# Second layer norm's variance taken from the first one's, and new orders of work for four of five blocks

## The reference, cut to what matters

```python
x = x + ssm(_gn(x))        # in_proj, 3x3 conv, 4 selective scans of 256 steps, 96 channels, 16 states
t = to_tokens(x)
t = t + attn(_ln_t(t))     # 12 heads of 16, causal
t = t + ffn(_ln_t(t))      # begins: h = _ln(t, g, b); attention over all tokens; MLP; 4 experts, top 2

def _ln_t(v, eps=1e-05):
    m = mean(v); s = var(v)
    return (v - m) / sqrt(s + eps)
```

## Time and profile before

| | |
|---|---|
| median of 3 runs | 740.43 us (737.93 to 743.23) |
| profiled execution, its own time | 742.85 us |
| its span | 741.1 us |
| TensorE busy | 608.1 us, 82% |
| VectorE busy | 516.4 us, 70% |
| ScalarE busy | 321.5 us, 43% |
| GpSimd busy | 201.3 us, 27% |

### The profile page before, as it was taken

How to read it: one execution, slowest core, us unless ns; L and a number is a source line. 1 busy time by engine, 2 the same in 40 slices (tenths; PEclk the granted TensorE clock), 3 DMA queues, 4 the chain that set the end, 5 groups by cost and what they waited for, 6 DMA issues and landing times. The chain is left out here.

```text
span 741.1 us, 9169 instructions
## 1 busy us (share of the span) xinstructions
PE 608.1 (82%) x3378; PEld 392.0 (53%) x3378; DVE 516.4 (70%) x986; ACT 321.5 (43%) x588; POOL 201.3 (27%) x158
## 2 busy tenths in 40 slices
PE   3899947898737689958898789867996989898897
PEld 2232225455212576645455576645465767676696
DVE  3869746868998578789997478799995465542311
ACT  2334202236353053784572345583761324672241
POOL 4449710005474201053442010153441001000000
PEclk9999968689768799878999789889999999999999
DMA  6375940348772002386750004575620000000000
GB/s 130 40 178 145 278 141 0 44 99 206 185 188 60 11 0 38 80 200 155 178 134 0 22 0 57 144 187 147 181 63 11 0 2 1 0 1 11 1 1 11
DMA packets 26642, 61.70 MB, mean 83 GB/s; under 512 B 4928, under 2 KB 12752, under 8 KB 26608
## 3 DMA queue, kind: packets, MB, share of 16 engines
q1 hardware_dynamic: 26608, 61.26, 34.8%
HBM read 53.52 MB, written 3.54 MB: 77 GB/s over the span
## 5 line engine op out<-in xcount | busy, mean ns | idle before, releaser
L1106 PE MATMUL pd<-w_dn,act 128*128 128x192 f32 x480 | 87.2, 336 | 5.5 <-ACT act L1872 3.7
L1992 POOL TENSOR_TENSOR state<-state,C_rows 128x1024 f32<-128x1024 f32 x24 | 69.8, 2909 | 62.5 <-DVE state L1491 40.6
L1106 PEld LDWEIGHTS pd<-w_dn,act 128*128 128x128 f32 x480 | 80.2, 195 | 11.7 <-issue 6.3
L1090 PE MATMUL pu<-fT,w_up 128*128 128x256 f32 x180 | 61.8, 427 | 7.6 <-ACT act L1872 7.6
L1967 POOL TENSOR_TENSOR norm_rstd<-norm_var,half 128x2 f32<-128x2 f32 x20 | 14.0, 698 | 197.5 <-DVE norm_var L1304 197.5
L1872 ACT ACTIVATE act<-pu,b_up 128x256 f32<-128x256 f32 x90 | 37.7, 470 | 67.4 <-PE pu L1094 67.2
L942 PE MATMUL py<-identb 128*32 128x512 bf16 x224 | 59.1, 412 | 0.0
L1842 ACT ACTIVATE decay<-d_rows,a_neg 128x255 f32<-128x255 f32 x96 | 40.5, 498 | 11.2 <-DVE state L1491 10.3
L1092 PE MATMUL pu<-fT_high,w_up_stack 128*128 128x256 f32 x90 | 45.2, 503 | 0.0
L1032 PE MATMUL py<-state,sel 128*32 128x512 f32 x96 | 43.8, 665 | 1.6 <-POOL state L1992 1.6
L822 PE MATMUL ps<-hT,w_qkv 96*96 96x256 f32 x128 | 35.9, 444 | 9.5 <-ACT hT L1902 8.6
(11 more groups left out here) (310 smaller groups left out, 1384.6 us busy)
## 6 DMA issues: line engine op xcount, KB each, us to landing
dx_rows<-delta_x_dram SPq DMA_DIRECT2D x41, 512.0 KB, 5.2
d_rows<-delta_dram SPq DMA_DIRECT2D x36, 512.0 KB, 6.3
d_rows<-delta_x_dram SPq DMA_DIRECT2D x6, 512.0 KB, 4.8
w_dn<-exp_w_dram SPq DMA_DIRECT2D x1, 2304.0 KB
B_rows<-xdbl SPq DMA_DIRECT2D x4, 512.0 KB, 6.9
C_rows<-xdbl SPq DMA_DIRECT2D x4, 512.0 KB, 10.5
delta_x_dram<-delta_x SPq DMA_DIRECT2D x4, 384.0 KB, 3.4
w_up<-exp_w_dram SPq DMA_DIRECT2D x1, 1536.0 KB
```

Of the source, the lines that this page charges most:

```text
L1090: nc.tensor.matmul(out, w_up[:, e, hidden], fT[:, :], start=True, stop=False)
L1106: mm = nc.tensor.matmul(pd[:, WIDTH * tl:WIDTH * (tl + 1)], act[e % 2][:, m, 128 * tl:128 * (tl + 1)], w_dn[:, e, m, :], start=(m == 0), s ...
L1992: nc.gpsimd.tensor_tensor(now, now, C_rows[:, :], ALU.mult).then_inc(sc_done, 1)
```

## The change

It has two parts. In the seam, `norm(3)` loses its statistics. When rstd of norm 2 is there, VectorE forms var * rstd * rstd (which is s / (s + eps)) and adds eps, with three instructions on 128x2 numbers, and GpSimd takes the power of it while VectorE applies norm 2. h_tok is then v_tok times that number, without a shift:

```diff
-                            link(norm(2, lambda tl: x2[:, tl, :], lambda tl: v_tok[:, tl, :]))
-                            norm(3, lambda tl: v_tok[:, tl, :], lambda tl: h_tok[:, tl, :]).then_inc(h_done, 1)
+                            norm_stats(2, lambda tl: x2[:, tl, :])
+                            dve.wait_ge(rstd_done[2], 1)
+                            link(nc.vector.tensor_tensor(norm_twice[:, :], norm_mv[:, 2, :, 1],
+                                                         norm_rstd[:, 2, :], ALU.mult))
+                            link(nc.vector.tensor_tensor(norm_twice[:, :], norm_twice[:, :],
+                                                         norm_rstd[:, 2, :], ALU.mult))
+                            nc.vector.tensor_scalar(norm_var[:, 3, :], norm_twice[:, :], EPS, None,
+                                                    ALU.add).then_inc(var_done[3], 1)
+                            link(norm_apply(2, lambda tl: x2[:, tl, :], lambda tl: v_tok[:, tl, :]))
+                            dve.wait_ge(rstd_done[3], 1)
+                            for tl in range(TILES):
+                                ins = nc.vector.tensor_scalar(h_tok[:, tl, :], v_tok[:, tl, :],
+                                                              norm_rstd[:, 3, tl:tl + 1], None, ALU.mult)
+                            ins.then_inc(h_done, 1)
```

The other part is new tables for OPENING, FIRST, STEADY and LAST. SyncE's order is the same as before. In OPENING the rows of VectorE, ScalarE and GpSimd are the same too, and dummy matmuls move on TensorE. A few lines of the tables:

```diff
 FIRST "PE"
-        (0, "spread"): [("keep_busy", 19)],
-        (0, "output"): [("keep_busy", 30)],
+        (0, "context"): [("keep_busy", 6)],
+        (0, "output"): [("keep_busy", 27)],
 FIRST "POOL"
-        (1, "context"): [("y_norm",), ("split_up", 4)],
-        (1, "output"): [("y_out",), ("split_up", 5)],
+        (1, 8): [("split_up", 4), ("split_up", 5)],
+        (1, "context"): [("times_C", 11), ("y_norm",)],
+        (1, "output"): [("y_out",)],
 STEADY "PE"
-        (0, "spread"): [("ffn_up", 1, 2)],
-        (0, "output"): [("ffn_down", 1, 0), ("ffn_up", 2, 0), ("ffn_up", 2, 1)],
-        (1, "turned"): [("ffn_up", 2, 2)],
+        (0, "context"): [("ffn_turn_gates",), ("keep_busy", 15)],
+        (0, "spread"): [("ffn_bias",)],
+        (0, "output"): [("ffn_up", 1, 2), ("ffn_down", 1, 0), ("ffn_up", 2, 0), ("ffn_up", 2, 1)],
+        (1, "turned"): [("keep_busy", 17), ("ffn_up", 2, 2)],
 LAST "PE"
-        (1, "spread"): [("ffn_down", 4, 0), ("ffn_down", 4, 1)],
+        (1, "context"): [("ffn_down", 4, 0), ("ffn_down", 4, 1)],
```

More of the change, by code:

```diff
@@ L223 @@
[L223 to L229 removed]
+        (0, "turned"): [("ffn_turn", 0), ("x_turn",)],
@@ L244 @@
         (1, "projected"): [("scan", 3)],
[L245 to L254 removed]
+        (1, 0): [("scan", 4), ("scan", 5), ("ffn_add", 1)],
@@ L255 @@
+        (1, 1): [("scan", 6)],
+        (1, 3): [("scan", 7), ("scan", 8)],
+        (1, 4): [("ffn_add", 2), ("scan", 9)],
+        (1, 5): [("scan", 10)],
+        (1, 6): [("ffn_add", 3)],
+        (1, 7): [("scan", 11)],
+        (1, 10): [("y_copy",), ("y_norm",)],
+        (1, "spread"): [("y_turn",), ("ffn_add", 4), ("y_out",)],
     },
     "ACT": {
-        (0, 0): [("ffn_up", 0, 0)],
-        (0, 1): [("ffn_up", 0, 1), ("ffn_up", 0, 2), ("in_proj",), ("x_dbl", 0)],
-        (0, 3): [("x_dbl", 1)],
@@ L289 @@
+        (1, "context"): [("y_out",)],
     },
```

393 lines of the change are left out of this document (192 added, 201 removed).

## The result

The kernel after takes 746.25 us (median of 20 runs, 741.97 to 755.99), the kernel before 741.65 us in its 20 runs (737.48 to 752.83). The ratio is 1.006 with a 95% interval of 1.0042 to 1.0077: some 4.4 us slower (3.1 to 5.7). A few executions of either kernel take about 1% longer at a lower granted clock, and all ratios here are of the others. The forecast was 731.7 us, its range ended at 742. The profiled execution of after took 745.71 us, with a span of 744.0 us; that of before 742.85 and 741.1.

What follows compares the result with a forecast made beforehand. No engine alone bounds the kernel; a block is as long as a chain that changes engines. FIRST -2.2, STEADY -5.8 and LAST -0.7 make -8.7 us, from the median 740.43 to 731.7 us, range 724 to 742.

Steps and rivals of the forecast that it cites:

- The seam: Between the attentions: h_tok without second statistics is ready 1.5 us sooner; at most 6.0 us over four places.
- -0.7 at the end of the round: STEADY: the faster norm gains 0.7 us per round, between 0 and 1.5, only if ScalarE comes sooner.
- Rival A: Norm's gain hidden under ScalarE's and TensorE's queues, barrier not waiting for the store: 737.4 us, chance 0.30.
- 27 dummies: FIRST's seam: 27 instead of 30 dummies take 6.0 us, so TensorE reaches the transposes sooner: -0.65 us.
- I let the two cancel: STEADY's end: ffn_down 4 ahead of y_turn and y_out (2.1 us each part) against sums coming earlier: net zero.
- The store: STEADY's end: store lands before the sum into v, step to next block 3.8 to 1.6 us: -2.2 per round.
- -2.9 per round: STEADY: -0.7 from the norm and -2.2 from the store in each round, -5.8 over two rounds.
- forecast at -2.2: FIRST as a whole: -0.65 at the seam, -1.55 from the shifts and 0 for its first half.
- -1.55 from the shifts: FIRST's end: two shifts fall from 0.94 to 0.16 us once GpSimd's products lie earlier; bounds 0 and -1.6.
- from -2 to +2: FIRST's first half: fewer dummies free about 1 us, later in_proj delays the convolution up to 1.7 us; taken as 0.
- rival B: New dummies in STEADY stand in the way, 7.9 us exposed per round: 749.6 us, chance 0.12.
- C: Dummies at STEADY's seam keep the clock up, q, k, v matmuls 3.3 instead of 6.67 us: 726.7 us, chance 0.13.

Runs made afterwards that it cites:

- e1: Kernel before with the new seam norm alone, all tables as before; ratio 0.9992 (0.9953 to 1.0031).
- e4: Kernel before with only STEADY's round end changed: ffn_down 4 1 ahead of y_turn, ffn_add 4 ahead of y_out; ratio 0.9954 (0.9926 to 0.9981).
- e6: Kernel after with ffn_up 4 2 behind the last two sums over states in STEADY; ratio 1.0126 (1.0063 to 1.0188).
- e9: New seam and new STEADY table alone, other tables as before, with 22 of a round's 79 dummies taken out; ratio 1.0039 (1.0004 to 1.0074).
- e3: Kernel after with the 11 dummies of before put back around y_sum 11 at FIRST's end; ratio 1.0097 (1.006 to 1.0133).
- e5: Kernel after with 7 dummies of before put back in STEADY's first half; ratio 1.0095 (1.0054 to 1.0136).
- e2: Kernel after with the old double norm, all new tables kept; ratio 1.0147 (1.0087 to 1.0208).
- e7: Kernel before with the new seam and the new table for STEADY alone; ratio 1.0037 (0.9991 to 1.0084).
- e8: Kernel before with new seam, STEADY's early store and new LAST; OPENING and FIRST as before; ratio 0.9945 (0.9902 to 0.9988), 739.4 us.
- e10: Kernel after with FIRST's in_proj at its old slot, ahead of the scores; ratio 1.016 (1.0094 to 1.0226), from four runs.
- e11: Kernel after with 11 dummies in FIRST ahead of the eleventh sum over states; ratio 1.0027 (0.9991 to 1.0063).
- e12: Like e8, with FIRST's last two 64x384 GpSimd products moved between its last products with C; ratio 0.9924 (0.9897 to 0.9952), 736.46 us.
- e16: Like e12, with the old double norm; ratio 0.9946 (0.9905 to 0.9988).

## Why the prediction was wrong

**The seam** was right in its mechanism (1.65 us measured, 1.5 forecast, and the two engines don't take turns), and its "-0.7 at the end of the round" was too much for the old order: 0.1 to 0.3 in e1. Rival A described that part. In FIRST I had the 27 dummies right (6.00 us). I had not priced that 6 dummies ahead of the projection run at the lower clock: 0.5 us for the projection.

**The step that failed first** is "I let the two cancel" at the end of a STEADY round. The store gave 1.9 us, 2.2 forecast. Against it I set nothing, and two terms were there. y_copy came 1.8 and 1.5 us later behind GpSimd's last product, because TensorE reached the last sums late: its list has no wait in the 39.5 us ahead of y_copy, with 26 dummies in it. And from y_copy to the sum into v it was 0.5 us longer, with ffn_down 4 1 ahead of y_turn; by itself that move costs 1.3 to 1.7 us (e4). My reason, that the sums now come ahead of "ffn_up 4 2's neighbours", misread the tables: they stand behind ffn_up 4 2 in both, and with them ahead of it (e6) y_copy was no sooner. That the full list is what makes the sums late is argued from the windows and from e9, whose y_copy came 4.8 and 4.6 us behind the product with 13 dummies there; no ratio shows it.

From residual sum to the sum into v after is 1.0 and 1.3 us longer than before in spite of the faster norm, where I had -0.7. A round, in after less before, adds up so:

| part of a round | round 1 | round 2 | forecast |
|---|---|---|---|
| start to the seam's residual sum | +4.4 | -2.3 | 0 |
| from there to GpSimd's first product | -1.2 | -0.8 | -0.7 |
| first product to last | -0.1 | 0 | 0 |
| last product to y_copy | +1.8 | +1.5 | 0 |
| y_copy to the sum into v | +0.5 | +0.5 | 0 |
| that sum to the next block | -1.9 | -1.9 | -2.2 |

So -2.9 per round became +3.5 and -3.0. The prediction named this sign: wrong if STEADY is not shorter by 2 us per round, or if FIRST comes out longer. Both happened.

**FIRST**, forecast at -2.2, was +1.4 in this profile: the residual sum came 0.5 us later, GpSimd's first product 0.7 sooner behind it, its chain from first to last product was 1.2 longer (61.4 instead of 60.2 us, with the two weight products inside it), y_copy came 1.6 us later behind the last product, and the -1.55 from the shifts came as -1.3 (y_copy to the sum into v 11.6 us instead of 12.9). The convolution began 0.9 us later, the projection behind 6 dummies took 0.5 us longer. I had set the first half at 0 "from -2 to +2", and the longer chain and the later sum had no term. The block also moves by itself: with the new table and the new seam it was 149.7, 150.0, 150.2 and 150.3 us (after, e3, e5, e6), with the new table and the old seam 146.9 (e2); with the table of before it was 148.3, 146.2, 145.8, 147.0 and 149.9 (before, e1, e4, e7, e8). The means of these five and five are 149.4 and 147.4.

**The clock** was in rival B and C, with the wrong place. The dummies at the seam kept it up, as C said (3.69 us instead of 6.67). That is no chance of one execution: the q, k, v projection behind the seam takes 3.69 us in both rounds of all twelve profiles with the new table, and 6.55 to 6.79 in the six with the old one. The scans did not get shorter by it: from GpSimd's first product to its last 66.4 us in after, 66.5 in before. That step was right. The 1.2 and 0.8 us by which they began sooner reached GpSimd's last product and were lost behind it, on TensorE. By that reading B was right in kind, with 1.5 to 1.8 us a round where it had 7.9.

**Not foreseen at all** was TensorE's code being loaded again at the jump back to the second round: some 2.3 us on the average of the executions, and none in the six profiles with the old table. With it, a rough sum from profiles: +0.5 in OPENING, +2.0 in FIRST, -1.5 in the two rounds of STEADY from the residual sums on, -0.4 in LAST (108.7 us, the mean of after, e2, e3, e5 and e6, against 109.1), -0.3 in CLOSING (60.5 against 60.8), and +2.1 in the first halves of the two rounds, where the residual sum comes 64.1 and 61.6 us into the round (means of after, e2, e3, e5, e6, e7, e10 and e11) against 61.5 and 62.0 (before, e1, e4, e8, e12 and e16). That makes 4.7 us, beside 4.4 measured. Since single blocks differ by 2 us and more between executions of one list, that they agree is in part luck.

What stays open: the rest of the 3 us that the new norm is worth in the new STEADY table, what makes the second round's code stay in some executions, why the slow sum in FIRST is more frequent, and how far the two clock stretches of round 1 come from the tables. In the twelve profiles with the new table the projection of round 1 started between 59.9 and 63.7 us, in the six with the old one between 58.4 and 61.0, so a part of it may.

## What to carry to other kernels

Ask of every instruction that is moved ahead of a wait what the engine will be doing at the moment when the wait ends; a store put early is paid for by the matmuls that must then come early too. Before you believe a difference of blocks between two profiles, look at the same block in two executions of one list: here they lay 2 to 5 us apart by TensorE's clock alone, as much as any edit gave. And before you add dummies, ask whether the engine still has a wait to put them in: here TensorE had none left in the 39.5 us ahead of y_copy, and it came late to the sums that the chain waited for.
